# A prologue loaded in halves, with two of six key and value chunks projected behind the first scores

## The reference

```python
x = x + tanh(g_xattn[0]) * attention0(layernorm(x), ctx)
# attention0(latents, context): 32 query heads, 8 key/value heads, head width 128
kv = concat([context, latents], axis=1)              # 768 rows a batch
q, k, v = latents @ Wq, kv @ Wk, kv @ Wv             # in heads
q, k = rms_norm(q) * q_norm_w, rms_norm(k) * k_norm_w
out = softmax(q k^T / sqrt(128)) v                   # 4 query heads share a k/v head
return out @ Wo
```

## Time and profile before

| what | us |
|---|---|
| median of 3 runs | 1005.25 (1004.34 to 1007.79) |
| the profiled execution, device time | 1001.03 |
| its span in the trace | 999.1 |
| TensorE busy | 955.8 (96%) |
| VectorE busy | 643.4 (64%) |
| ScalarE busy | 479.3 (48%) |
| GpSimd busy | 356.0 (36%) |

### The profile page before, as it was taken

One profiled execution on the slowest core, in us unless ns is written; L12 is line 12 of the kernel. 1 busy time (PEld: TensorE's weight loads), 2 busy tenths in 40 slices (PEclk: granted clock), 3 DMA queues, 4 the chain that ended last, 5 costly groups with the idle time before them and its releaser, 6 DMA issues. The chain is left out here.

```text
span 999.1 us, 18524 instructions
## 1 busy us (share of the span) xinstructions
PE 955.8 (96%) x6876; PEld 828.9 (83%) x6876; DVE 643.4 (64%) x1102; ACT 479.3 (48%) x937; POOL 356.0 (36%) x244
## 2 busy tenths in 40 slices
PE   4989999999999999999999999999989998999996
PEld 3879989998998899899989989898967777777755
DVE  5567557656755774675577467556734875788856
ACT  4356336534643653464356346535614512566644
POOL 3335317243541633344154324423134620170033
PEclk9989999999999999999999999999999998899999
DMA  6020203201210220032021102100134304843001
GB/s 231 1 65 32 55 1 84 63 0 22 73 53 0 84 52 11 0 94 53 0 74 29 44 0 84 63 0 11 22 91 164 114 13 149 200 59 64 2 1 43
DMA packets 40677, 55.01 MB, mean 55 GB/s; under 512 B 8640, under 2 KB 20544, under 8 KB 40640
## 3 DMA queue, kind: packets, MB, share of 16 engines
q1 hardware_dynamic: 40064, 54.49, 20.0%
q10 hardware_dynamic: 576, 0.00, 0.0%
HBM read 50.22 MB, written 4.26 MB: 55 GB/s over the span
## 5 line engine op out<-in xcount | busy, mean ns | idle before, releaser
L440 DVE TENSOR_TENSOR ptL<-tbank,ptH 128x512 fp32r<-128x512 f32 x192 | 132.2, 689 | 69.4 <-ACT ptH L309 66.9
L309 ACT ACTIVATE ptH<-tbank 128x512 fp32r<-128x512 f32 x192 | 115.5, 601 | 110.9 <-PE tbank L556 110.5
L556 PE MATMUL tbank<-ident,probs 128*128 128x128 f32 x864 | 132.7, 276 | 6.7 <-DVE ptL L440 3.4
L453 DVE TENSOR_REDUCE negmax<-score 128x1 f32<-128x768 f32 x128 | 120.4, 950 | 10.8 <-PE score L80 10.3
L330 ACT ACTIVATE probs<-score,negmax 128x768 f32<-128x768 f32 x128 | 115.5, 903 | 18.3 <-DVE negmax L453 18.3
L78 PE MATMUL obank<-ptH,vH 128*128 128x256 f32 x384 | 121.4, 316 | 0.0
L411 DVE TENSOR_REDUCE sumsq<-probs 128x2 f32<-128x256 f32 (+1 forms) x80 | 42.0, 526 | 115.4 <-ACT probs L304 71.8
L556 PEld LDWEIGHTS tbank<-ident,probs 128*128 128x128 f32 x864 | 97.9, 140 | 17.5 <-DVE ptL L440 10.2
L217 POOL TENSOR_TENSOR rnorm<-sumsq,neg_half 128x2 f32<-128x2 f32 (+1 forms) x80 | 71.4, 895 | 107.8 <-DVE sumsq L413 107.7
L80 PE MATMUL obank<-ptH,vL 128*128 128x256 f32 x384 | 108.8, 283 | 0.0
L80 PE MATMUL score<-wkvH,kvT_lo 128*128 128x256 f32 x384 | 108.7, 283 | 0.0
(11 more groups left out here) (263 smaller groups left out, 2249.6 us busy)
## 6 DMA issues: line engine op xcount, KB each, us to landing
wqo_stage<-in_wq SPq DMA_DIRECT2D x9, 1024.0 KB, 5.4
wqo_stage<-in_wo SPq DMA_DIRECT2D x8, 1024.0 KB, 7.2
factors<-r_scratch SPq DMA_DIRECT2D x32, 256.0 KB, 4.0
wkv_stage<-in_wkv SPq DMA_DIRECT2D x9, 512.0 KB, 6.2
a_qS<-q_scratch SPq DMA_DIRECT2D x24, 128.0 KB, 5.3
ctx_stage<-in_ctxT SPq DMA_DIRECT2D x2, 1024.0 KB, 13.2
kS<-k_scratch SPq DMA_DIRECT2D x32, 64.0 KB, 3.5
q_scratch<-qpart SPq DMA_DIRECT2D x16, 128.0 KB, 1.9
```

Source lines behind the costliest of these rows:

```text
L309: act.activation(out, tbank[c % 2][:], ACT.Copy, scale=scale).then_inc(t_hi, 1)
L440: i = dve.tensor_tensor(out, tbank[c % 2][:], f32(hi), ALU.subtract)
L453: dve.tensor_reduce(negmax[:, m:m + 1], score[m % 2][:, 0:SKV], AX.X, ALU.max, negate=True).then_inc(s_max, 1)
L556: i = pe.transpose(tbank[c % 2][:, n * P:(n + 1) * P], block_in, S.ident[:])
```

## The change

- The rows x and the first query weights are each loaded by two transfers of half the size. Statistics, 1/sqrt and normalisation go tile by tile: GpSimd has eight one-column instructions for the former two of four columns.
- ScalarE makes each block of `wqH` behind the high part of one row tile. VectorE makes `wqL` blocks 0 and 1 between the low parts of the row tiles, GpSimd blocks 2 and 3.
- In the prologue TensorE projects chunks 0 to 3 of keys and values, transposes q0, k0 and k1, makes `scores(0, 0)`, then projects chunks 4 and 5 into the banks `obank` (rows of keys into `o_norm`), and transposes k2. The other engines' lists are reordered in the same way.
- `exp(g, 0)` and `exp(g, 1)` stand at the end of `prepare` and not at the start of `attend`, so that ScalarE has the same order as before in the turns, with the loop's jump behind and not ahead of them.
- Two semaphores of the second attention are dropped.

```diff
-            sp.dma_start(S.X[:], A.x.rearrange("b (t p) d -> p (b t) d", p=P)).then_inc(x_in, 16)
-            S.load_wq(sp, 0)
+            for half in (slice(0, 2), slice(2, 4)):
+                sp.dma_start(S.X[:, half, :], A.x.rearrange("b (t p) d -> p (b t) d", p=P)[:, half, :]).then_inc(x_in[half.start // 2], 16)
+            for half in (slice(0, 2), slice(2, 4)):
+                sp.dma_start(S.wqo_stage[:, half, :], A.wq0.rearrange("(t p) n -> p t n", p=P)[:, half, 0:GRP * D0]
+                             ).then_inc(wq_piece[half.start // 2], 16)
...
+    EARLY = 4
+
+    def kv_bank(c, first):
+
+        return obank[c - EARLY][:] if first and c >= EARLY else pbank[c % 4]
+
+    def k_tiles(c, first):
+
+        if first and c >= EARLY:
+            return o_norm[:].rearrange("p (t d) -> p t d", d=D0)[:, 2 * (c - EARLY):2 * (c - EARLY) + 2, :]
+        return k_rows[:, 2 * c:2 * c + 2, :]
...
-            pool.wait_ge(stats_done, 2 * RT)
-            rsqrt_rows(pool, rstd[:], mv[:, :, 1], LN_EPS, S.neg_half[:, 0:RT], rstd_step)
-            for k in range(KT):
+            for t in range(RT):
+                pool.wait_ge(stats_done, 2 * t + 2)
+                rsqrt_rows(pool, rstd[:, t:t + 1], mv[:, t, 1:2], LN_EPS, S.neg_half[:, 0:1], rstd_step, 2 * t)
+            for k in range(KT // 2, KT):
                 pool.wait_ge(wq_hi, k + 1)
                 i = pool.tensor_tensor(wqL[:, k, :], S.wqo_stage[:, k, :], f32(wqH[:, k, :]), ALU.subtract)
-            i.then_inc(wq_split, 2)
+            i.then_inc(wq_split, 1)
...
             def split_inputs():
-                act.wait_ge(S.wq_in, 16)
-                for k in range(KT):
-                    act.activation(wqH[:, k, :], S.wqo_stage[:, k, :], ACT.Copy).then_inc(wq_hi, 1)
                 for t, tile in enumerate(LATENT_TILES):
                     act.wait_ge(tr_done, t + 1)
                     act.activation(S.kvH[:, :, tile * P:(tile + 1) * P],
                                    tbank[t % 2][:].rearrange("p (k n) -> p k n", k=KT), ACT.Copy).then_inc(hi_done, 1)
+                    act.wait_ge(wq_piece[t // 2], 16)
+                    act.activation(wqH[:, t, :], S.wqo_stage[:, t, :], ACT.Copy).then_inc(wq_hi, 1)
...
             def attend(g):
-                exp(g, 0)
-                exp(g, 1)
...
                 hi_q(g, 0)
                 for i in range(3):
                     hi_k(g, i)
+                exp(g, 0)
+                exp(g, 1)
...
-            for c in range(NKV):
-                evac_kv(0, c)
-            prepare(0)
+            for c in range(EARLY):
+                evac_kv(0, c, True)
+            hi_q(0, 0)
+            hi_k(0, 0)
+            hi_k(0, 1)
+            exp(0, 0)
+            exp(0, 1)
+            for c in range(EARLY, NKV):
+                evac_kv(0, c, True)
+            hi_k(0, 2)
             turns(act, turn, last)
...
             def split_inputs():
-                dve.wait_ge(x_in, 16)
-                layernorm_stats(dve, S.X, stats, mv, stats_done)
-                dve.wait_ge(rstd_step, 2)
-                for t in range(RT):
-                    dve.tensor_scalar(xn[:, t, :], S.X[:, t, :], mv[:, t, 0:1], rstd[:, t:t + 1],
-                                      ALU.subtract, ALU.mult).then_inc(xn_done, 1)
+                for t in range(RT + 1):
+                    if t < RT:
+                        dve.wait_ge(x_in[t // 2], 16)
+                        dve.bn_stats(stats[:, t, :], S.X[:, t, :]).then_inc(stats_done, 1)
+                        dve.wait_ge(stats_done, 2 * t + 1)
+                        dve.bn_aggr(mv[:, t, :], stats[:, t, :]).then_inc(stats_done, 1)
+                    if t:
+                        dve.wait_ge(rstd_step, 2 * t)
+                        dve.tensor_scalar(xn[:, t - 1, :], S.X[:, t - 1, :], mv[:, t - 1, 0:1], rstd[:, t - 1:t],
+                                          ALU.subtract, ALU.mult).then_inc(xn_done, 1)
                 for t, tile in enumerate(LATENT_TILES):
+                    if t >= 2:
+                        dve.wait_ge(wq_hi, t - 1)
+                        i = dve.tensor_tensor(wqL[:, t - 2, :], S.wqo_stage[:, t - 2, :], f32(wqH[:, t - 2, :]), ALU.subtract)
+                        if t == 3:
+                            i.then_inc(wq_split, 1)
                     dve.wait_ge(hi_done, t + 1)
...
-            fill_items(0, 0)
+            fill_items(0, 0, RT + EARLY, True)
             lo_q(0, 0)
-            for i in range(3):
-                lo_k(0, i)
+            lo_k(0, 0)
+            lo_k(0, 1)
             maximum(0, 0)
             maximum(0, 1)
+            fill_items(0, RT + EARLY, NIT, True)
+            lo_k(0, 2)
             turns(dve, turn, last)
...
-            project_kv(0)
+            project_kv(0, range(EARLY), True)
             transpose_q(0, 0)
-            for i in range(3):
-                transpose_k(0, i)
+            transpose_k(0, 0, True)
+            transpose_k(0, 1, True)
             scores(0, 0)
+            project_kv(0, range(EARLY, NKV), True)
+            transpose_k(0, 2, True)
             turns(pe, turn, last)
```

More of the change, by code:

```diff
@@ L196, in _, with split @@
         def _(pool):
-            def split(hi, lo, stage, arrived, g, done):
-                pool.wait_ge(arrived, 16 * g + 16)
+            def split(hi, lo, stage, arrived, count, g, done):
+                pool.wait_ge(arrived, 16 * count)
                 zero = S.zero[:].unsqueeze(1).to_broadcast(list(stage.shape))
@@ L204, in split_wq @@
             def split_wq(g):
-                split(wqH[:], wqL[:], S.wqo_stage[:], S.wq_in, g, wq_split)
+                split(wqH[:], wqL[:], S.wqo_stage[:], S.wq_in, g + 1, g, wq_split)
             def split_wkv(g):
-                split(wkvH[:], wkvL[:], S.wkv_stage[:], S.wkv_in, g, wkv_split)
+                split(wkvH[:], wkvL[:], S.wkv_stage[:], S.wkv_in, g + 1, g, wkv_split)
             def split_wo(g):
-                split(woH[:], woL[:], S.wqo_stage[:], S.wo_in, g, wo_split)
+                split(woH[:], woL[:], S.wqo_stage[:], S.wo_in, g + 1, g, wo_split)
             def rsqrt_items(g):
@@ L259, in last @@
                 pool.wait_ge(pe_kv, NKV * LAST + NKV)
[L260 removed]
+                split(wkvH[:], wkvL[:], S.wkv_stage[:], S.wkv1_in, 1, 0, S.wkv1_split)
                 for h in range(2, GRP):
@@ L414, in sum_squares, with normalise @@
                                   ALU.mult, ALU.add).then_inc(ss_done, 1)
-            def normalise(g, it):
-                (rows, n), a = item(it), GRP * it
+            def normalise(g, it, first=False):
+                (rows, n), a = item(it, first), GRP * it
                 dve.wait_ge(rn_done, NIT * g + it + 1)
@@ L420, in normalise, with v_lo_part, fill_items @@
                                   ALU.mult).then_inc(normed, 1)
-            def v_lo_part(g, c):
-                kv = pbank[c % 4].rearrange("p (t n) -> p t n", t=2)
+            def v_lo_part(g, c, first=False):
+                kv = kv_bank(c, first).rearrange("p (t n) -> p t n", t=2)
                 dve.tensor_tensor(vL[:, 2 * c:2 * c + 2, :], kv[:, :, D0:2 * D0],
                                   f32(vH[:, 2 * c:2 * c + 2, :]), ALU.subtract).then_inc(v_lo, 1)
-            def fill_items(g, first):
-                for it in range(first, NIT):
+            def fill_items(g, start, stop=NIT, first=False):
+                for it in range(start, stop):
                     sum_squares(g, it)
                     if it >= RT:
[L431 to L434, removed]
+                        v_lo_part(g, it - RT, first)
+                    if it > start or start == 1:
+                        normalise(g, it - 1, first)
+                normalise(g, stop - 1, first)
             def lo(g, name, out, hi, scale=None):
@@ L534, in project_q, with project_kv @@
                 i.then_inc(pe_q, 1)
-            def project_kv(g):
+            def project_kv(g, chunks=range(NKV), first=False):
                 pe.wait_ge(wkv_split, NS * g + NS)
-                for c in range(NKV):
+                for c in chunks:
                     if c < 4:
                         pe.wait_ge(act_q, RT * g + c + 1)
-                    else:
+                    elif not first:
                         pe.wait_ge(v_lo, NKV * g + c - 3)
@@ L557, in transposes, with transpose_k @@
                 i.then_inc(pe_t, 1)
-            def transpose_k(g, i):
+            def transpose_k(g, i, first=False):
                 pe.wait_ge(normed, NIT * g + K_NORMED[i])
-                transposes(g, ("k", i), [k_rows[:, 4 * i + n, :] for n in range(4)])
+                transposes(g, ("k", i), [k_tiles(2 * i + n // 2, first)[:, n % 2, :] for n in range(4)])
             def transpose_q(g, h):
```

26 lines of the change are left out of this document (13 added, 13 removed).

## The result

The changed kernel is slower: median 1011.36 us (1002.67 to 1015.46, 20 runs) against 1004.16 us (998.31 to 1007.79, 20 runs) for the kernel before. The ratio is 1.0074, 95% interval 1.0053 to 1.0095, which is 7.4 us (5.3 to 9.5). The profiled execution took 1010.34 us with a span of 1008.5 us, 9.4 us over the span before.

A forecast was written before the change was run, and what follows sets the result against it. TensorE is busy for 88.47 of each 89 us turn, so only the first 60 us can win or lose. Start -0.4, second wait +4.0 and clock +1.6 give +5.2 us: 1010.4 us, range 1005.8 to 1014.0.

The forecast's parts named there:

- The start: Path up to the first projection: a gain of 0.4 us, bounds a loss of 0.3 and a gain of 3.7.
- the held case: At the start, VectorE's wqL block falls between or behind GpSimd's two; wq_split at about 17.4, gaining 0.2 to 0.3 us.
- the chain over the two banks: At the start, low part 0, tile 2's transposes, high part 2 and wqH block 2 let GpSimd start at 14.2 us.
- The hold: At the start, VectorE and GpSimd lock each other out on wqL: start at 17.5 us with it, 16.9 without.
- The wait for k1: Between last projection and first scores: not shortened, scores 6.17 us behind that projection, taking 4.00 us at the lower clock.
- The second wait: Behind chunk 5, the chain of 3.02 us stands again with nothing under it, ahead of k2's transposes; loss 4.0 us.
- held clock: Rival at 15%: the clock stays up in both prologue waits, kernel not slower, +0.8 us, 1006.1 us.
- The clock: Behind the new wait, a second fall to half clock slows the new scores: 1.6 us, between 0 and 2.4.
- a ready turn: First turn from the first tile of scores(0, 1), exponentials ready: 5.17 us against 6.30 before, giving 1.1 us.
- the loss of 4.0 us: From last projection before first scores into the first turn: 26.95 us against 22.92 before, ahead of the separate clock term.
- The place of the exponentials: Exponentials before the loop's jump cost nothing; rival at 4%: seven turns change by 0.5 us each, 1007 or 1014 us.
- The start at its ceiling: Rival at 9%: weights split as they land and no hold at the start, +1.9 us, 1007.2 us.

The follow-up runs named there:

- e5: Changed kernel with VectorE's two wqL blocks one behind the other, ahead of tile 2's low part; 1009.91 us in one execution.
- e1: Changed kernel's start alone, all six chunks projected ahead of the first scores again; median 1004.71 us, ratio 1.0003 to the kernel before.
- e3: Changed kernel with 31 spare matmuls filling TensorE's waits in the prologue; median 1005.92 us, ratio 0.9994 to the kernel before.
- e8: Kernel before with 13 spare matmuls in its one wait; median 1004.21 us, ratio 1.0009 to the kernel before.
- e2: Changed order of chunks alone, with the start of the kernel before; median 1011.74 us, ratio 1.0074.
- e6: e4 with k2's high and low parts ahead of first exponentials and second maximum, plus e5's edit; median 1001.38 us, ratio 0.9980 to the kernel before.
- e4: Changed kernel with late chunks 4 and 5 moved into the first wait; median 1001.96 us, ratio 0.9975 to the kernel before.

## Why the prediction was right, step by step

**The start: right, by the held case.** Forecast -0.4, measured -0.31. Three kernels with the old start begin at 17.74, 17.80 and 18.07 us, four with the new one at 17.43 to 17.82, so 0.3 us is the difference of their means too; but it is no more than their scatter, and to hit the tenth was in part luck. The half of the rows landed at 4.94 us (forecast 5.4). One column's power takes 0.57 us, where I had taken a third of 1.05, and the chain over the two banks delivered wqH block 2 at 14.3 (forecast 14.2). The hold was the open point. VectorE's block took 1773 ns against 683 for its first, and GpSimd's two took 1268 and 1727 ns, starting at 14.3 and 15.6 us. VectorE (from 14.38) stood until GpSimd's first ended at 15.6, then ran to 16.15, while GpSimd's second stood for it. e5 took the hold away by order alone. What I had weighed from the Trainium skill ("SBUF — State Buffer", who interferes with whom) is shown here for a subtraction with two SBUF operands as well. By that page's rule the second to issue is fully blocked, and so it went, once on either side: 1.09 us for VectorE, 0.45 us for GpSimd.

**A term that I left out: the slow pace of the first projections.** Their matmuls of 512 columns stood 0.43 us apart from 17.43 to about 23.1 us and 0.23 us apart from then on; before, the slow spell ended at 20.4 us. The changed kernel, then the one before:

```profile
22.25 0.63 PE L80 MATMUL score<-wqH,kvT_lo 128*128 128x512 f32 x1
22.68 0.63 PE L78 MATMUL score<-wqH,kvT_hi 128*128 128x512 f32 x1
...
23.62 0.39 PE L78 MATMUL score<-wqH,kvT_hi 128*128 128x512 f32 x1
23.84 0.39 PE L79 MATMUL score<-wqL,kvT_hi 128*128 128x512 f32 x1
```

```profile
20.01 0.63 PE L80 MATMUL score<-wqH,kvT_lo 128*128 128x512 f32 x1
20.44 0.51 PE L78 MATMUL score<-wqH,kvT_hi 128*128 128x512 f32 x1
...
21.02 0.39 PE L80 MATMUL score<-wqH,kvT_lo 128*128 128x512 f32 x1
```

The column of the granted clock says 1.00 here; 0.43 us is the spacing that matmuls of 512 columns have in the first scores too, where it says 0.50. From the first projection to the end of the chunks it is 25.18 us and two chunks at 2.88, so 30.94 against 29.64 before: +1.30 us. Ahead of it TensorE idled 3.47 us, before 0.58. It isn't chance of one execution: the seven profiled kernels with the new start, which all idle 3.0 to 3.5 us there, keep that pace for 4.0 to 5.7 us, the three with the old one (idle 0.3 to 0.6 us) for 1.4 to 3.1 us. That the idle time is the cause isn't shown; no run changed it alone. The term eats the start's gain. In e1 it is +1.33 us; there 0.24 from the start and 0.74 behind the chunks, where the clock was at half for 3.4 us (54.03 to 57.44) and not for 6.8, set it off to +0.35. I named the term only as an edge of the range.

**The wait for k1: right.** With T as in the prediction (the end of the last projection ahead of the first scores, 42.61 us here), it is hardly shortened: 5.87 us from T to the first scores against 6.17, the 0.3 less because the clock fell behind k1's transposes and not within them. The first scores took 4.01 us (forecast 4.00).

**The second wait: right.** From the scores' end to k2's transposes it took 9.46 us (forecast 9.2), then 2.16 us to the scores of batch 1 (forecast 2.34). The new idle times of 2.92 and 1.06 us have the releasers that I named. With the clock held in both kernels, the way from T to the same point of the first unit is 24.09 us in e3 (42.19 to 66.28; forecast for a held clock 24.15). So the loss against the kernel before is 1.17 us there (forecast for a held clock 1.23). In e8 the point is at 62.67, 15.04 us behind its T of 47.63. With the 5.76 us of the two chunks the second wait costs 24.09 - 15.04 - 5.76 = 3.3 us.

**The clock: right in kind, and worth more than it looked.** The last piece took 6.45 us against the 5.17 of a ready turn, 1.28 us (forecast 1.6). With the clock held (e3) that piece took 5.05 us. But the loss of 4.0 us that I had put down to waits already held some of the clock's price: with the clock held in both kernels it is 3.3. Taken apart by e3 and e8: the clock costs the changed kernel 27.95 - 24.09 = 3.86 us behind T, the kernel before 17.16 - 15.04 = 2.12. So of the 5.03 us lost behind T (27.95 against 22.92), 3.29 are the wait and 1.74 the clock. These are figures of single executions. The spells at half clock behind the same waits were 6.8 and then 3.4 us long in the changed kernel, 3.4 and then 6.8 in e2, and 6.8 before against 3.4 in e1, which took 0.74 us less behind T. And a reading of mine was wrong: I wrote that before the clock had held for 2.6 of the 2.79 idle us. It held through all of them and fell at 51.41 us, 0.20 us into the transposes.

**The sum.** -0.31 + 1.30 + 5.03 = +6.02 us in the prologue, forecast +5.2. The term left out (+1.30) is more than the difference; the pieces that I had put at +5.6 behind T came to 5.03, so two errors in part cancelled. Whole runs lost 7.4 us (5.3 to 9.5), which takes in the 6.02. The lower end of my range, 1005.8, was meant as the case of the held clock, whose sum gives 1006.1.

**What cost nothing.** The place of the exponentials: from the first to the last spreading it is 656.44 to 656.68 us in ten kernels, on either side of the loop's jump (before and e8 are the two with the old place, 656.51 and 656.44). I didn't try that edit alone.

**The rivals.** The held clock didn't come about by itself. Made by hand (e3) it gave a kernel within 0.3% of the one before, as that rival had it (+0.8 forecast, +1.74 in the prologue, -0.6 with -3.0 to +1.8 in whole runs). The start at its ceiling fell to the chain over the banks and to the hold. Nothing made the kernel faster.

**Open.** Behind the turns the same work took 273.9 to 285.4 us in ten profiled executions. The mean clock goes with it (0.998 and 0.980 at the two ends), and the place shows. This is TensorE from 830 to 870 us (us, busy, granted clock, DMA share, GB/s), in the kernel before and in e6:

```profile
830.00:870.00 40.00, 36.84 (x328) 0.83 0.83 214
```

```profile
830.00:870.00 40.00, 37.66 (x421) 1.00 0.88 217
```

In that stretch the granted clock is 1.00 in e1 and e6, whose ends are the shortest (274.1 and 273.9 us), and 0.79 to 0.83 in the other eight. Why it falls in some executions and not in others stays open; no run here changed that part. Such differences are large enough to hide that two prologues lie 1.9 us apart (before and e8).

## What to carry to other kernels

Work moved behind a dependent step to hide one wait brings its own chain of evacuation along; ask what covers that chain in its new place. Put such work into the wait that is already there, and then look at every engine's list for what now stands ahead of the part that TensorE waits for (behind T, e4 gained 2.1 us on the kernel before where e6, with k2's parts ahead of the exponentials, gained 4.0). A wait's idle time isn't its whole price: one that lets the clock fall is paid again in the work behind it.

## What the runs showed of the hardware

- Behind a single wait of 2.80 us between groups of transposes the granted clock fell to half, for 6.8 us, at the end of the four transposes that followed. In the other kernels with that wait (2.79 or 2.80 us) it fell 0.20 us into the transposes (before) or 0.50 us behind the last of eight (e1). Waits of 0.82, 1.13, 0.41 and 0.66 us (e6) left it at 1.00. In e3 spare matmuls in the four waits kept it at 1.00, and from k2 to the scores of batch 1 the time was the same to 0.01 us.
- A subtraction with two SBUF operands on VectorE and one on GpSimd that start 0.05 us apart hold each other in turn: 1773 ns in place of 683, and 2.95 us in place of 2.50 for GpSimd's two.
- The first matmuls of the kernel ran at the pace of the lower clock (0.43 us apart in place of 0.23) for 2.7 us before and 5.7 us after the change, while the granted clock stands at 1.00 in the profile there. At the start the spacing of matmuls is to be read, not that column.
- GpSimd's power takes 0.57 us for one column (once 0.72) and 1.05 us for four, so splitting it by tile more than doubles its work.
- A transfer of 512 KB at the start landed 4.2 us behind its issue, the 1 MB one 6.0 us.
